# Cross-attention: row maxima of five of thirteen score tiles subtracted by VectorE in PSUM instead of by matmuls

## The reference

```python
q = (x @ w_q).reshape(b, n, HEADS, DIM_HEAD)
kv = (context @ w_kv).reshape(b, m, 2, HEADS, DIM_HEAD)
k, v = (kv[:, :, 0], kv[:, :, 1])
attn = jnp.einsum('bnhd,bmhd->bhnm', q, k) * scale
attn = jax.nn.softmax(attn, axis=-1)
out = jnp.einsum('bhnm,bmhd->bnhd', attn, v).reshape(b, n, INNER)
return out @ w_out + b_out
```

## Time and profile before

| | us |
|---|---|
| median of 3 runs | 1943.23 |
| profiled execution, its time | 1947.53 |
| profiled execution, its span | 1945.8 |
| PE matmul busy | 1735.3 (89%) |
| DVE busy | 1169.5 (60%) |
| ACT busy | 830.2 (43%) |
| POOL busy | 1269.8 (65%) |
| cross-attention blocks, first to last score matmul | 259.2 to 1698.0 |

### The profile page before, as it was taken

How to read it: one execution, slowest core, us unless ns; L and a number is a source line. 1 busy time by engine, 2 the same in 40 slices (tenths; PEclk the granted TensorE clock), 3 DMA queues, 4 the chain that set the end, 5 groups by cost and what they waited for, 6 DMA issues and landing times. The chain is left out here.

```text
span 1945.8 us, 32715 instructions
## 1 busy us (share of the span) xinstructions
PE 1735.3 (89%) x10604; PEld 1209.3 (62%) x10604; DVE 1169.5 (60%) x2037; ACT 830.2 (43%) x1199; POOL 1269.8 (65%) x705
## 2 busy tenths in 40 slices
PE   6654799999989999998999999989999999826992
PEld 5544566666656666666666666656666666425991
DVE  4776455656565656666565656565666656674665
ACT  3223144444444445454444444444444444422223
POOL 3867248667676676676867667686676686526554
PEclk8876789999999999999999999999999999858996
DMA  6001300000200000010000000200000000232224
GB/s 194 1 22 33 120 1 23 1 23 0 77 1 23 1 24 23 0 55 23 23 1 23 3 22 0 77 1 23 1 23 23 0 16 1 76 119 92 74 76 144
DMA packets 39141, 71.24 MB, mean 37 GB/s; under 512 B 4632, under 2 KB 28568, under 8 KB 37728
## 3 DMA queue, kind: packets, MB, share of 16 engines
q1 hardware_dynamic: 35264, 59.27, 9.1%
q0 software_dynamic: 3744, 10.23, 1.7%
HBM read 55.97 MB, written 13.52 MB: 36 GB/s over the span
## 5 line engine op out<-in xcount | busy, mean ns | idle before, releaser
L1173 POOL TENSOR_TENSOR xa_total<-xa_total,xa_pexp 128x1024 f32<-128x1024 f32 (+1 forms) x341 | 831.8, 2439 | 62.2 <-ACT xa_pexp L1096 38.7
L1269 DVE TENSOR_REDUCE xa_parts<-ps_ring 128x1 f32<-128x402 f32 x1024 | 531.5, 566 | 266.8 <-PE ps_ring L1016 253.5
L1096 ACT ACTIVATE xa_pexp<-ps_s 128x1024 f32<-128x1024 f32 (+1 forms) x416 | 426.2, 1026 | 395.1 <-PE ps_s L970 357.3
L984 PE MATMUL ps_pv<-xa_pexp,xa_v 128*64 128x512 f32 (+1 forms) x1664 | 399.9, 604 | 0.0
L984 PEld LDWEIGHTS ps_pv<-xa_pexp,xa_v 128*64 128x64 f32 (+1 forms) x1664 | 106.1, 137 | 182.8 <-issue 141.0
L970 PE MATMUL ps_s<-xa_q_neg,xa_row_one 64*128 64x512 f32 (+1 forms) x832 | 180.6, 393 | 0.0
L1173 POOL TENSOR_TENSOR xa_total<-xa_pexp 128x1024 f32<-128x1024 f32 x31 | 74.0, 2386 | 160.9 <-ACT xa_pexp L1096 159.6
L1149 ACT COPY xa_v<-ps_ring 128x256 f32<-128x256 f32 (+1 forms) x208 | 77.5, 373 | 204.5 <-PE ps_ring L955 202.7
L1016 PE MATMUL ps_ring<-xa_k_hi,xa_q_hi 64*128 64x402 f32 x512 | 127.3, 378 | 6.1 <-DVE xa_parts L1269 5.2
L1016 PE MATMUL ps_ring<-first_k_hi,xa_q_hi 64*128 64x402 f32 x512 | 123.6, 388 | 3.4 <-DVE xa_q_lo L1263 1.5
L1223 POOL TENSOR_TENSOR first_wa_lo<-wa_raw,first_wa_hi 128x1536 fp32r<-128x1536 f32 x16 | 55.6, 3476 | 97.1 <-ACT first_wa_hi L1159 97.1
(11 more groups left out here) (302 smaller groups left out, 3370.1 us busy)
## 6 DMA issues: line engine op xcount, KB each, us to landing
wa_raw<-in_pack_a SPq DMA_DIRECT2D x17, 768.0 KB, 4.5
ex_raw<-in_pack_e SPq DMA_DIRECT2D x8, 1024.0 KB, 6.4
ctx_raw<-in_ctxT SPq DMA_DIRECT2D x4, 1601.0 KB, 8.7
wb_raw<-in_pack_b SPq DMA_DIRECT2D x16, 256.0 KB, 2.6
ex_w<-ybuf SPq DMA_DIRECT2D x8, 512.0 KB, 7.5
sa_xT<-in_xT SPq DMA_DIRECT2D x8, 256.0 KB, 6.1
X<-in_x SPq DMA_DIRECT2D x1, 2048.0 KB, 11.6
x_hi<-sa_x1s_hi SPq DMA_DIRECT2D x16, 128.0 KB, 2.1
```

The costliest lines, as they stand in the source:

```text
L984: ins = nc.tensor.matmul(ps_pv[half(h), :], v[0:m, t, at:at + XD], pexp[0:m, buf, h, :], start=t == 0, stop=t == MT - 1)
L1096: nc.scalar.activation(pexp[0:m, buf], ps_s[0:m, (p * MT + t) % 2], ACT.Exp, scale=XD ** -0.5)\
L1173: engine.tensor_tensor(total[p][0:m], first, pexp[0:m, buf], ALU.add).then_inc(s["add_done"], 1)
L1269: nc.vector.tensor_reduce(parts[:, h, q, c:c + 1], ps_ring[:, r, 0:CW], AX.X, ALU.max)\
```

## The change

In a block with `VECTOR_SHIFTS` = (3, 5, 7, 9, 11), the score tiles of these t leave out the fourth pair of matmuls. DVE adds in its place `wide_max[p]`, a copy of the negated maxima on all partitions, to the tile in PSUM, in place (128 x 1024), and ACT's exponential of the tile waits for that (`shifted`) instead of for PE. The copy is made once a block by a new ring job `BC`, twice (one for each head), at the end of t = 1: a matmul of `row_one` and `q_neg` on 64 rows into a bank, and an ACT copy of 128 x 512 from it into SBUF. All blocks have it but the first block of rounds 3, 7 and 11 and both blocks of round 15. `wide_max` lies in the buffers of the experts' raw weights, so the loads of experts 0 and 1 move from the prologue to SP's queue at t = 0 of the last round (`LDX`), behind a wait for the last addition.

```diff
 RING = 3
-RING_JOBS = ("K", "Q", "MX", "SH", "V", "RS", "OP", "TX", "GT")
+RING_JOBS = ("K", "Q", "MX", "SH", "BC", "V", "RS", "OP", "TX", "GT")
...
+VECTOR_SHIFTS = (3, 5, 7, 9, 11)
...
-def block(p, more, maxima, tail):
+def block(p, more, maxima, tail, shifts=VECTOR_SHIFTS):
...
-        steps.append(("S", p, t))
+        steps.append(("S", p, t, "DVE") if t in shifts else ("S", p, t))
...
         steps.extend(behind)
+        if t == 1 and shifts:
+            steps += [("BC", p, 0), ("BC", p, 1)]
...
+    if last:
+        loads = join(loads, {0: ([("LDX", 0), ("LDX", 1)], [])})
+    steps = block(0, join(own, loads, {} if first else chain(1, 1)), maxima_of(1), tail, () if last or batch_ends else VECTOR_SHIFTS)
...
-        for e in range(STG):
-            self.load(sp, a, e)
...
+        wide_max = [ahead.raw[p][:, 0:2 * N] for p in range(2)]
...
+                elif kind == "LDX":
+                    if st[1] == 0:
+                        need(sp, s["shifted"], n.of("VS"))
+                    ahead.load(sp, a, st[1])
...
# PE
+                    passes = 3 if st[-1] == "DVE" else 4
...
-                                                  (k_hi[p][:, ms], q_lo[p]), (row_one[:, 0:m], q_neg[p]))):
+                                                  (k_hi[p][:, ms], q_lo[p]), (row_one[:, 0:m], q_neg[p]))[:passes]):
...
+                elif kind == "BC":
+                    p, h = st[1:]
+                    r = take_bank(n)
+                    nc.tensor.matmul(ps_ring[:, r, :], row_one[half(h), :], q_neg[p][half(h), :], start=True, stop=True)\
+                        .then_inc(filled[r], 1)
...
# ACT
+                    if st[-1] == "DVE":
+                        act.wait_ge(s["shifted"], n.of("VS") + 1)
+                    else:
+                        act.wait_ge(s["scores_ready"], n.of("S") + 1)
...
+                elif kind == "BC":
+                    p, h = st[1:]
+                    r = n.slot()
+                    act.wait_ge(filled[r], n.of("ring%d" % r) + 1)
+                    nc.scalar.copy(wide_max[p][:, h * N:(h + 1) * N], ps_ring[:, r, :]).then_inc(drained[r], 1)
...
# DVE
+                elif kind == "S" and st[-1] == "DVE":
+                    p, t = st[1:3]
+                    m = rows(t)
+                    dve.wait_ge(s["scores_ready"], n.of("S") + 1)
+                    r, c = n.job(("BC", p, 1))
+                    dve.wait_ge(drained[r], c)
+                    nc.vector.tensor_tensor(ps_s[0:m, (p * MT + t) % 2].rearrange("p h n -> p (h n)"),
+                                            ps_s[0:m, (p * MT + t) % 2].rearrange("p h n -> p (h n)"), wide_max[p][0:m], ALU.add)\
+                        .then_inc(s["shifted"], 1)
```

More of the change, by code:

```diff
@@ L657, in one_round @@
         loads = join(loads, {0: ([], [("ST", 0)]), 3: ([], [("ST", 1)]), 11: ([], [("ST", 2)])})
-    steps = block(0, join(own, loads, {} if first else chain(1, 1)), maxima_of(1), tail)
+    if last:
+        loads = join(loads, {0: ([("LDX", 0), ("LDX", 1)], [])})
+    steps = block(0, join(own, loads, {} if first else chain(1, 1)), maxima_of(1), tail, () if last or batch_ends else VECTOR_SHIFTS)
     if last:
@@ L665, in one_round @@
                            9: ([], [("GT", 2), ("GT", 3), ("TX", 4), ("TX", 5)]), 11: ([], [("GT", 4), ("GT", 5)])})
-        return steps + block(1, join(chain(0, 0, at=5), head), [], end)
+        return steps + block(1, join(chain(0, 0, at=5), head), [], end, ())
     nxt = {1: ([], [("K", 0, 2), ("K", 0, 3)]), 6: ([], [("WB",)])}
@@ L690, in keys @@
             out.append("COPY")
+        if st[-1] == "DVE":
+            out.append("VS")
         if st[0] in RING_JOBS:
@@ L863, in cross_attention @@
         s.update(loads.sems)
-        s.update(sems(ctx, nc, "fin_inv fin_att fin_hi fin_lo stats_done"))
+        s.update(sems(ctx, nc, "fin_inv fin_att fin_hi fin_lo stats_done shifted"))
         ah = ahead.sems
         xT_g = [negmax[:].rearrange("p c n -> p (c n)"), total[0][:, 0, :]]
+        wide_max = [ahead.raw[p][:, 0:2 * N] for p in range(2)]
         filled = [s[f"filled{r}"] for r in range(RING)]
@@ L960, in handle @@
                 if kind == "S":
-                    p, t = st[1:]
+                    p, t = st[1:3]
+                    passes = 3 if st[-1] == "DVE" else 4
                     if t == 0:
@@ L967, in handle @@
                     for q, (kk, qq) in enumerate(((k_hi[p][:, ms], q_hi[p]), (k_lo[p][:, ms], q_hi[p]),
-                                                  (k_hi[p][:, ms], q_lo[p]), (row_one[:, 0:m], q_neg[p]))):
+                                                  (k_hi[p][:, ms], q_lo[p]), (row_one[:, 0:m], q_neg[p]))[:passes]):
                         for h in range(2):
                             ins = nc.tensor.matmul(ps_s[0:m, t_of(n), h, :], kk[half(h)], qq[half(h), :],
-                                                   start=q == 0, stop=q == 3)
+                                                   start=q == 0, stop=q == passes - 1)
                     ins.then_inc(s["scores_ready"], 1)
@@ L1089, in handle @@
                 if kind == "S":
-                    p, t = st[1:]
-                    act.wait_ge(s["scores_ready"], n.of("S") + 1)
+                    p, t = st[1:3]
+                    if st[-1] == "DVE":
+                        act.wait_ge(s["shifted"], n.of("VS") + 1)
+                    else:
+                        act.wait_ge(s["scores_ready"], n.of("S") + 1)
                     m, buf, prev = rows(t), pexp_buffer(t), user_before(p, t)
```

## The result

The changed kernel takes 2026.97 us (median of 4 runs, 2022.81 to 2028.5) against 1943.97 for the kernel before on the same chip (4 runs, 1942.93 to 1945.23): a ratio of 1.0423, 95% interval 1.041 to 1.0436. (Ratios here are the record's own estimates; the quotient of the two medians differs from them by up to 0.001.) It is slower by 83 us. The prediction was 2005 (1957 to 2035), slower with 0.80.

What follows compares the result with a forecast made beforehand. PE was taken to bound the kernel; first blocks +35, second blocks +27 and round 0 -0.3 us gave +61 on the profiled 1947.5, so 2009, and 2005 for the median, range 1957 to 2035, slower with 0.80.

Steps and rivals of the forecast that it cites:

- 135 x 0.235 = 32 us off PE: Five score tiles in 27 blocks: each removed matmul pair saves PE 0.235 us, 32 us in all.
- the second MX of tile t waits for the first reduction of tile t - 1: Tiles 4 to 9, first block with a chain: dependency holding PE 0.7 us at tile 7 and 1.9 at tile 9.
- was to gain 0.3: First block of round 0, without a chain: hides its additions, +0.6 - 4 x 0.235 = -0.3 us.
- BC's 0.6 us a block: Ring at t = 1 and 2: BC makes tile 4 start 0.6 us later, +16 us in 27 blocks, from 0 to 27.
- the +2.8: First blocks with a chain, tiles 4 to 9: tile 10 starts at 18.25 instead of 15.47 us, bounds +2.2 and +3.7.
- The clock falls: Rival: lower clock in tiles 9 and 10 of 26 chained blocks, +36 us on top, 2041; chance 0.08.
- The argument from the row of 3.86 us: PE's clock fell behind 3.86 us of idleness at a batch's end; new waits, up to 1.9, leave it alone.
- +1.4: Second blocks, tiles 4 to 9: tile 10 starts at 21.0 instead of 19.61 us, bounds -0.7 and +2.3.
- the moved loads at 0: Two 1 MB transfers moved from the prologue to t = 0 of the last round: cost 0, or 6.4 us uncovered.
- The sum of 61: Whole kernel: 35 us from first blocks, 27 from second blocks, -0.3 from round 0's first block.
- the rival that DVE hides the additions: Chain's tiles: reductions run late without holding the ring; faster, 1918, or 1934 if BC's wait stays; chance 0.15.
- that only first blocks suffer: Rival: second blocks hide their additions, -5 us, sum +30, 1973; mild end of the own case, which has 0.72.

Runs made afterwards that it cites:

- `pe_only`: Kernel before without the fourth matmul pair at five tiles of 27 blocks, no copy or addition in its place: 1944.28 us against 1949.16, ratio 0.9977.
- `bc_only`: Changed kernel with the two BC jobs kept, but four matmul pairs in all tiles and no additions: 1971.51 us against 1949.16 before, ratio 1.0113.
- `chain_tiles`: Changed kernel with the additions at tiles 5, 7 and 9 alone: 2038.82 us against 1949.16 for the kernel before, ratio 1.0458.
- `keep_clock`: Changed kernel, first MX matmul of tile 9 issued eleven times in the 11 first blocks with a chain: 2019.14 us against 1947.38 before, ratio 1.0361.
- `outside`: Changed kernel with the additions at tiles 3 and 11 alone: 1968.2 us against 1949.16 for the kernel before, ratio 1.0098.
- `late_tiles`: Changed kernel with BC at t = 0 and additions at tiles 10, 11, 12 alone, in 30 blocks: 2026.9 us against 1947.38 before, ratio 1.0405.

## Why the prediction was right, and where not

The sign and the mechanism stood: additions among the chain's reductions hold the ring, and PE waits for `xa_parts` at the second `MX` of tile 9. That the time fell inside the range owes something to luck: some terms were too small and others too large, and without the 11 us by which second blocks did better than forecast, the kernel would have been at about 2038, above the range's 2035. By its own terms:

1. **"135 x 0.235 = 32 us off PE" failed.** This is the wrong step. `pe_only` shows 4 to 5 us. Where a stretch takes two pairs of `MX` with three banks, the second pair has to wait for a round trip that the first pair started (from PE to DVE and back about 1.0 us, 881.52 to 882.53 above), and the next score tile of four pairs with its first `MX` was about that long (722.10 to 723.20). The text even stated the dependency ("the second MX of tile t waits for the first reduction of tile t - 1") and then booked every removed pair in full. The clearest row of it: round 0's first block, without a chain, was to gain 0.3 and got 0.64 longer, with tiles 4 to 9 at 13.15 before and after. Tile 11 gave 0.12 of its 0.235.
2. **BC's 0.6 us a block was 0.88 in the mean.** The forecast's own terms, 1.25 - 0.3 - 0.235, make 0.7 and not 0.6. The wait at `MX` came where it had been put, and seven of the 11 first blocks of `bc_only` lose 0.67 to 0.76 us; second blocks lose nearly 0.9, since the next ring job waits in turn, and four first blocks 1.2. In the changed kernel round 9 loses 3.3 us. There PE waits 1.32 us behind tile 1 (0.96 before), and from 1122.3 to 1129.1, between tiles 1 and 4, the granted clock is at the lower level, which it isn't in this place in the kernel before or in `chain_tiles`, where the round loses 1.1. Together tiles 0 to 3 cost 26 us instead of 16.
3. **First blocks, tiles 4 to 9: the +2.8 was +3.2 where the clock held, +4.48 in the mean.** From the start of tile 4 the forecast had R2 begin at 11.3 (measured 11.16) and the `MX` of tile 9 at 13.2 (14.18); tile 10 at 18.25 (18.64). The wait was 2.77 instead of 1.9, since R2 took 2.47 where 1.41 had been taken from a mean. Behind it the forecast was too long, 5.05 us to tile 10 instead of 4.46: R4 took 0.68 where 1.5 had been booked.
4. **"The clock falls" (0.08) came true in part:** not in 26 blocks but in 8 of 11 first blocks, where the mean is 20.30 against 18.53 in the other three: 8 x 1.77 = 14 us, with some 2 us more at the start of round 9. In rounds 9 and 12 the lower level lasted twice as long as in the other six. `keep_clock` shows that with PE at work in most of the wait the clock falls more rarely. In second blocks, whose longest wait here is 0.45, the clock stays at 1.00. The argument from the row of 3.86 us was right in kind and left no size between that and a few tenths.
5. **Second blocks, tiles 4 to 9: +1.4 was +0.67.** R2 took 0.69 there, where the forecast had 1.41 and the kernel before 1.80: this part of DVE's queue got 1.1 us shorter while the additions made it longer. The three removed pairs, booked at 0.7, shortened nothing (`pe_only`), so the forecast's waits, 2.1 us in sum, were too long by 1.4.
6. **Held:** the additions (1.2 forecast, 1.216 measured), their harmlessness at 3 and 11 (`outside`), DVE's busy time (1330 forecast, 1311.8), the moved loads at 0 (first block of the last round 37.82 us against 37.83), POOL's busy time (1266.5 against 1269.8).

The sum of 61 had to be 82. Its parts missed by +10 (BC), +18 (first blocks, 14 of it the clock), -11 (second blocks), +3 (tile 10 to the end) and +1 (round 0). In the rival that DVE hides the additions, 1934 doesn't follow from its terms: 27 x 0.33 on top of 1918 is 1927. Nothing else hangs on it.

The rival that DVE hides the additions is refuted by `chain_tiles` and `late_tiles`; that only first blocks suffer, by the +1.43 of second blocks, of which 0.88 is `BC`.

Open: why the clock fell after eight of 11 waits of the same length, and why the rounds behind a batch's end (4, 8 and 12) lose 1.2 to 1.3 us at their start. One rival stands untested: how much of the +3.2 is R2 meeting POOL, and not the additions' own time. R2 stood 1.8 us behind POOL (2.47 against 0.69), so an estimate from these rows is that without that PE's wait of 2.77 would be about 1.0. It was read from rows, and no run moves R2 or POOL's addition alone.

## What to carry to other kernels

Before booking removed matmuls as time, look for the round trip of a small ring in the same stretch: if the next bank comes free just when the removed work would have ended, PE waits instead. An engine that is 60% busy can be full in the stretch that counts, and even its half idle stretches may have the idle part at their end; cut the stretch once more before moving work there. Take a duration from the place in question and not from the mean of its group, above all for a DVE operation with both inputs in SBUF beside a working POOL.

## What the runs showed of the hardware

**R2 is as long as POOL makes it.** Durations of its 31 instances, before and after (ns, least, median, most):

```profile
L1329 DVE TENSOR_TENSOR xa_att<-xa_pv_sb,xa_inv x31: 692/1793/1960, 319.2 to 1685.9; 128x512 f32<-128x512 f32 x31
```

```profile
L1365 DVE TENSOR_TENSOR xa_att<-xa_pv_sb,xa_inv x31: 692/705/2484, 321.6 to 1768.0; 128x512 f32<-128x512 f32 x31
```

The means, 1411 and 1453 ns, are lengths that hardly one of them has. Before, R2 takes 0.81 to 0.87 us in first blocks with a chain and 1.79 to 1.91 in second ones; after, 2.46 to 2.48 and 0.69 or 0.70. In round 5 and round 6 of the kernel after, R2 ends 0.55 us behind the end of the POOL addition that had begun before it (757.94 and 757.39; 852.31 and 851.76). The same holds for all 30 instances of the kernel before that began while POOL was adding: 0.55 or 0.56 us behind POOL's end, whether 0.26 us of the addition were left or 1.41. R2 isn't slowed down in proportion, it stands still until POOL is through; in most second blocks of the kernel after at most 0.12 us of the addition are left, and it runs in 0.69. The Trainium skill (SBUF — State Buffer, "Who interferes with whom") says so: a DVE instruction with two SBUF inputs contends with a GpSimd instruction that reads SBUF, and the lock on the ports that they share is exclusive. These rows agree, and so do the additions in PSUM, with one SBUF input: 1.20 to 1.23 us in all 135, with POOL at work 63% of the span. What counts is which moment of POOL's additions R2 meets, not how late it is: the change moved it 1.6 us back in first blocks, from the last 0.3 us of an addition to 0.43 us behind the start of one, and 1.15 us back in second blocks, from the middle of an addition to its end. The first cost 1.65 us, the second gave 1.1, and no count of DVE's own work has either.

**The clock.** After 2.77 us of idleness the granted clock fell in 8 of 11 cases (in `chain_tiles`, after the same wait, in 10 of 11). After 1.00 us it didn't fall in 8 of 11 (`keep_clock`, round 6 among them), but in rounds 10, 13 and 14 it did. After the waits of up to 0.45 in the 15 second blocks it never fell. So the length of the last wait alone doesn't decide. The loss in round 6 is 1.25 us on the next 8 PV matmuls (3.19 against 1.94) and 1.5 by the start of tile 10. The prediction had weighed the profile's row, by which the new waits leave the clock alone, against the rule of the Trainium skill (TensorE: Matmul & The Clock Gate, "A second HAM failure mode: psum-queue depth-cycling"), by which a PE that idles briefly between groups while it cycles through PSUM banks can swing between the two levels; the truth lay between.
